# A token tower's finish rearranged: runs of sixteen tokens per partition, with base and weights sent through DRAM

## What is computed

```
h = _L0_tok_ref(x, ...)
h = h + _L0_attn_ref(_layernorm(h), ...)
h = h + _L0_ffn_ref(_layernorm(h), ...)     # = h + (xf + y)
# in _L0_ffn_ref, with xf the normalised tokens:
probs = softmax(xf @ Wr + br);  topk_w, topk_idx = top_k(probs, 2)
topk_w = topk_w / max(topk_w.sum(-1), 1e-9)
y = sum over the token's 2 experts e of  topk_w[e] * (gelu(xf @ W1[e] + b1[e]) @ W2[e] + b2[e])
```

## Time and profile before

| | us |
|---|---|
| median of three runs | 203.77 (203.3 to 203.94) |
| profiled execution, its own time | 204.18 |
| its span, first to last instruction | 202.4 |
| mean granted clock of TensorE | 0.875 of full |

### The profile page before, as it was taken

The page is one execution under the profiler, slowest core; times in us unless marked ns, Lnnn a source line. Parts: engine busy times, 40 slices in busy tenths (PEclk is TensorE's granted clock), DMA queues, the critical chain, the costliest instruction groups (busy, mean ns, idle before and its releaser), DMA issues.

```text
span 202.4 us, 3206 instructions
## 1 busy us (share of the span) xinstructions
PE 139.4 (69%) x792; PEld 100.0 (49%) x792; DVE 86.1 (43%) x289; ACT 74.5 (37%) x224; POOL 112.2 (55%) x154
## 2 busy tenths in 40 slices
PE   0429979999899566936189079999999999910000
PEld 0314324564565354535074059878777999910000
DVE  4261030454585485292698202545433322310183
ACT  2102124426444071130403035656566677700330
POOL 4293003130538777877777304777777777775250
PEclk9999999999999995795579856999999999995555
DMA  3999999999999921011011122444444421000877
GB/s 110 329 372 369 306 365 388 387 387 384 387 385 313 322 121 53 27 49 55 31 43 53 47 60 75 112 109 120 117 109 113 119 64 42 10 10 13 227 196 198
DMA packets 28948, 35.31 MB, mean 174 GB/s; under 512 B 3019, under 2 KB 18551, under 8 KB 28804
## 3 DMA queue, kind: packets, MB, share of 16 engines
q1 hardware_dynamic: 26328, 30.84, 47.3%
q0 software_dynamic: 2560, 4.27, 6.7%
q10 hardware_dynamic: 44, 0.01, 0.0%
HBM read 11.35 MB, written 24.81 MB: 179 GB/s over the span
## 4 chain that ended last, share of the span: by engine, by line
PE 45%; POOL 21%; issue 10%; DVE 10%; DMA 7%; ACT 2%; SPq 1%; ACTq 1%; DVEq 0%; POOLq 0%
PE bank L1075 13%; POOL slots L471 12%; PE bank L1065 11%; PE bank L919 9%; POOL parts L485 3%; PE bank L1052 3%; PE bank L904 3%; DMA work_a<-parts 3%; PE bank L909 3%; POOL root L456 2%; DVE work_c L854 2%; DMA rows<-in_L_tok_conv_b_dram 2%; POOL root_tab L421 1%; DMA slots<-stage,slot_of 1%; POOL root L464 1%
## 5 line engine op out<-in xcount | busy, mean ns | idle before, releaser
L485 POOL DMA_INDIRECT parts<-work_d,xt x48 | 47.2, 983 | 24.8 <-DVE work_d L837 16.0
L471 POOL DMA_INDIRECT slots<-stage,slot_of x32 | 32.4, 1011 | 11.0 <-issue 10.7
L585 ACT ACTIVATE act_hT<-bank,tile_b 128x128 f32<-128x128 f32 x96 | 30.1, 364 | 20.6 <-PE bank L1065 20.4
L1075 PE MATMUL bank<-w_sb,act_hT 128*128 (+1 forms) x192 | 32.8, 295 | 1.6 <-issue 0.6
L1075 PEld LDWEIGHTS bank<-w_sb,act_hT 128*128 128x128 f32 x192 | 26.0, 196 | 7.4 <-issue 6.9
L837 DVE TENSOR_TENSOR work_d<-bank,fb_bc 128x128 f32<-128x128 f32 x48 | 14.0, 292 | 35.9 <-PE bank L1075 35.9
L919 PE MATMUL bank<-x1T,convw_sb 128*128 128x512 f32 x48 | 23.2, 628 | 0.6 <-ACT x1T L532 0.4
L1065 PE MATMUL bank<-xtT,tile_w 128*128 128x128 f32 x128 | 21.4, 294 | 0.3 <-issue 0.3
L1065 PEld LDWEIGHTS bank<-xtT,tile_w 128*128 128x128 f32 x128 | 18.5, 209 | 0.6 <-issue 0.5
L1052 PE MATMUL bank<-ident,xt 128*128 128x128 f32 x48 | 13.9, 290 | 6.2 <-DMA xt<-slots 6.2
L575 ACT ACTIVATE xtT<-bank 128x128 f32<-128x128 f32 x48 | 13.3, 278 | 9.7 <-PE bank L1052 9.7
(11 more groups left out here) (181 smaller groups left out, 220.5 us busy)
## 6 DMA issues: line engine op xcount, KB each, us to landing
slots<-zero_rows SPq DMA_DIRECT2D x3, 4224.0 KB, 29.6
slots<-zero_rows SPq DMA_DIRECT2D x1, 5280.0 KB, 17.3
xt<-slots SPq DMA_DIRECT2D x48, 66.0 KB, 1.9
w_sb<-in_L_ffn_W_dram SPq DMA_DIRECT2D x1, 2048.0 KB, 16.7
fb_bc<-in_L_ffn_b_dram SPq DMA_DIRECT2D x1, 1024.0 KB, 7.0
work_b<-parts SPq DMA_DIRECT2D x4, 256.0 KB, 4.0
work_a<-parts SPq DMA_DIRECT2D x4, 256.0 KB, 5.8
out_dram<-work_c SPq DMA_DIRECT2D x4, 256.0 KB, 2.4
```

What stands on the lines that cost most here:

```text
L471: pool.indirect_dma_start(out=slots, out_offset=bass.IndirectOffsetOnAxis(ap=slot_of[:, g, k, s:s + 1].bitcast(U32), axis=0), in_=stage[:, ...
L485: pool.indirect_dma_start(out=parts, out_offset=bass.IndirectOffsetOnAxis(ap=xt[:, u, ROW_PLACE:ROW_PLACE + 1].bitcast(U32), axis=0), in_= ...
L585: last = act.activation(act_hT[:, b, c, :], bank[2 + b][:, c * P:(c + 1) * P], ACT.Gelu, bias=tile_b1[:, c, j:j + 1])
L1075: last = pe.matmul(bank[5 + j % 2][:, 0:D], act_hT[:, b, c, :], flat(w2_sb[:, expert_of(j), c, :]), start=(c == 0), stop=(c == 1))
```

## The change

The finish now gives each partition 16 tokens in a row (token 16 p + r), 8 KB of DRAM, in `CHUNKS` = 4 chunks of four tokens (2 KB per partition). `base` and `w_top` have the other layout, so SP writes them to DRAM tensors `base_rows` and `w_rows` ahead of its load of tile 16, and reads them back in the new layout, into `h1T` and `w_run`, ahead of its load of tile 32. First choices are loaded from SP's queue, second choices from ACT's. ACT scales all 16 blocks by w1; DVE computes base + w0 * first for all 16; POOL adds the two results for three chunks, DVE for the last.

```diff
+        w_run = sb("w_run", [P, T // P, TOPK])
...
+        RUN = T // P
+        CHUNKS = 4
+        CROWS = RUN // CHUNKS
+        base_run, first_run, second_run, scaled_run, sum_run, out_run = h1T, work_a, work_b, work_c, h0T, base
+
+        def run_rows(ap, c):
+
+            return ap.rearrange("(p r) d -> p (r d)", p=P)[:, c * CROWS * D:(c + 1) * CROWS * D]
+
+        def load_parts(eng, k, buf):
+
+            for u in range(U):
+                eng.wait_ge(placed[u], 16 * (TILES // U))
+            for c in range(CHUNKS):
+                eng.dma_start(buf[:, c, :], run_rows(parts[k * T:(k + 1) * T, :], c)).then_inc(parts_in[k][c], 16)
...
                 if j == 0:
                     sp.wait_ge(rows_out, 16 * TOPK * SEQS)
+                if j == U:
+                    sp.wait_ge(base_sum, GROUPS)
+                    sp.dma_start(base_rows.rearrange("(b p) d -> p b d", p=P),
+                                 base[:].rearrange("p g (s d) -> p (g s) d", d=D)).then_inc(base_out, 16)
+                    sp.wait_ge(w_ready, 1)
+                    sp.dma_start(w_rows.rearrange("(b p) k -> p b k", p=P), w_top[:]).then_inc(base_out, 16)
+                if j == FULL:
+                    sp.wait_ge(base_out, 32)
+                    sp.dma_start(base_run[:].rearrange("p g n -> p (g n)"),
+                                 base_rows.rearrange("(p r) d -> p (r d)", p=P)).then_inc(base_in, 16)
+                    sp.dma_start(w_run[:].rearrange("p r k -> p (r k)"),
+                                 w_rows.rearrange("(p r) k -> p (r k)", p=P)).then_inc(base_in, 16)
                 if j >= U:
                     sp.wait_ge(placed[u], 16 * (j // U))
                 sp.dma_start(xt[:, u, :], slots[bass.ds(row, P), :]).then_inc(xt_in[u], 16)
...
-            for k, buf in ((1, work_b), (0, work_a)):
-                for g in range(GROUPS):
-                    sp.dma_start(by_seq(buf[:, g, :]), both[k, :, g * GS:(g + 1) * GS, :]).then_inc(parts_in[k][g], 16)
+            load_parts(sp, 0, first_run)
+            tokens = out.rearrange("b t d -> (b t) d")
+            for c in range(CHUNKS):
+                sp.wait_ge(y_out, c + 1)
+                sp.dma_start(run_rows(tokens, c), out_run[:, c, :]).then_inc(stored, 16)
...
-            for g in range(GROUPS):
-                pool.wait_ge(scaled_y, g + 1)
-                most = slice(0, (GS - 1) * P)
-                pool.tensor_tensor(work_d[:, g, most], work_c[:, g, most], base[:, g, most], ALU.add).then_inc(summed, 1)
+            for c in range(CHUNKS - 1):
+                pool.wait_ge(scaled_y, c + 1)
+                pool.wait_ge(summed, c + 1)
+                pool.tensor_tensor(out_run[:, c, :], scaled_run[:, c, :], sum_run[:, c, :], ALU.add).then_inc(y_out, 1)
...
+            load_parts(act, 1, second_run)
+            act.wait_ge(base_in, 32)
+            for c in range(CHUNKS):
+                act.wait_ge(parts_in[1][c], 16)
+                for i in range(CROWS):
+                    last = act.activation(blocks(scaled_run[:, c, :], i), blocks(second_run[:, c, :], i), ACT.Copy,
+                                          scale=w_run[:, c * CROWS + i, 1:2])
                 last.then_inc(scaled_y, 1)
...
+            dve.wait_ge(base_in, 32)
+            for c in range(CHUNKS):
+                dve.wait_ge(parts_in[0][c], 16)
+                for i in range(CROWS):
                     last = dve.scalar_tensor_tensor(
+                        out=blocks(sum_run[:, c, :], i), in0=blocks(first_run[:, c, :], i),
+                        scalar=w_run[:, c * CROWS + i, 0:1], in1=blocks(base_run[:, c, :], i), op0=ALU.mult, op1=ALU.add)
+                last.then_inc(summed, 1)
+            dve.wait_ge(summed, CHUNKS)
+            dve.wait_ge(scaled_y, CHUNKS)
+            dve.wait_ge(y_out, CHUNKS - 1)
+            dve.tensor_tensor(out_run[:, CHUNKS - 1, :], scaled_run[:, CHUNKS - 1, :], sum_run[:, CHUNKS - 1, :],
+                              ALU.add).then_inc(y_out, 1)
```

More of the change, by code:

```diff
@@ L63, in tower_kernel @@
     parts = nc.dram_tensor("parts", [TOPK * T, D], F32).ap()
+    base_rows = nc.dram_tensor("base_rows", [T, D], F32).ap()
+    w_rows = nc.dram_tensor("w_rows", [T, TOPK], F32).ap()
     with ExitStack() as ctx:
@@ L231, in tower_kernel @@
         onehot_tile, b1_psum, b1_ready, t_w1 = map(sem, ("onehot_tile", "b1_psum", "b1_ready", "t_w1"))
+        w_ready, base_out, base_in = map(sem, ("w_ready", "base_out", "base_in"))
         parts_in = [[sem(f"parts{k}_in{g}") for g in range(GROUPS)] for k in range(TOPK)]
-        base_sum, base_ready, stored, scaled_y, summed, y_out = map(sem, ("base_sum", "base_ready", "stored", "scaled_y", "summed", "y_out"))
+        base_sum, stored, scaled_y, summed, y_out = map(sem, ("base_sum", "stored", "scaled_y", "summed", "y_out"))
         def blocks(ap, s):
@@ L371, in _ @@
                 sp.dma_start(xt[:, u, :], slots[bass.ds(row, P), :]).then_inc(xt_in[u], 16)
-            for u in range(U):
-                sp.wait_ge(placed[u], 16 * (TILES // U))
-            both = parts.rearrange("(k b p) d -> k p b d", k=TOPK, p=P)
-            for k, buf in ((1, work_b), (0, work_a)):
-                for g in range(GROUPS):
-                    sp.dma_start(by_seq(buf[:, g, :]), both[k, :, g * GS:(g + 1) * GS, :]).then_inc(parts_in[k][g], 16)
-            tokens = out.rearrange("b t d -> t b d")
-            for g in range(GROUPS):
[L382 to L385, removed]
+            load_parts(sp, 0, first_run)
[3 more added lines that the diff above has]
+                sp.dma_start(run_rows(tokens, c), out_run[:, c, :]).then_inc(stored, 16)
+            sp.wait_ge(stored, 16 * CHUNKS)
         @block.gpsimd
@@ L589, in _ @@
             experts(gelu=gelu, evacuate_x=evacuate_x)
-            act.wait_ge(base_ready, 1)
-            for g in range(GROUPS):
-                act.wait_ge(parts_in[1][g], 16)
-                for s in range(GS - 1):
-                    last = act.activation(blocks(work_c[:, g, :], s), blocks(work_b[:, g, :], s), ACT.Identity,
-                                          scale=w_top[:, g * GS + s, 1:2])
+            load_parts(act, 1, second_run)
[5 more added lines that the diff above has]
+                                          scale=w_run[:, c * CROWS + i, 1:2])
                 last.then_inc(scaled_y, 1)
@@ L840, in _ @@
             experts(load_expert=load_expert, add_b2=add_b2, copy_w1=copy_w1)
-            dve.wait_ge(base_ready, 1)
-            for g in range(GROUPS):
-                dve.wait_ge(parts_in[1][g], 16)
-                last = dve.scalar_tensor_tensor(
-                    out=blocks(work_d[:, g, :], GS - 1), in0=blocks(work_b[:, g, :], GS - 1),
-                    scalar=w_top[:, g * GS + GS - 1, 1:2], in1=blocks(base[:, g, :], GS - 1), op0=ALU.mult, op1=ALU.add)
-            link(last)
-            for g in range(GROUPS):
-                dve.wait_ge(parts_in[0][g], 16)
-                dve.wait_ge(summed, g + 1)
-                for s in range(GS):
-                    last = dve.scalar_tensor_tensor(
-                        out=blocks(work_c[:, g, :], s), in0=blocks(work_a[:, g, :], s), scalar=w_top[:, g * GS + s, 0:1],
-                        in1=blocks(work_d[:, g, :], s), op0=ALU.mult, op1=ALU.add)
-                last.then_inc(y_out, 1)
+            dve.wait_ge(base_in, 32)
+            for c in range(CHUNKS):
+                dve.wait_ge(parts_in[0][c], 16)
+                for i in range(CROWS):
+                    last = dve.scalar_tensor_tensor(
+                        out=blocks(sum_run[:, c, :], i), in0=blocks(first_run[:, c, :], i),
[6 more added lines that the diff above has]
+                              ALU.add).then_inc(y_out, 1)
         @block.tensor
```

4 lines of the change are left out of this document (1 added, 3 removed).

## The result

The changed kernel takes 215.48 us in the median of four runs (213.69 to 215.94), the kernel before in the same comparison 203.54 us (four runs). The ratio is 1.0588, 95% interval 1.0501 to 1.0674: slower, and beyond the range. The profiled execution took 215.18 us, its span is 213.4 us (before 202.4).

| stretch | before, us | changed, us | difference |
|---|---|---|---|
| start to the first scatter to `parts` | 122.98 | 122.37 | -0.6 |
| first to last scatter (48 tiles) | 61.64 | 70.54 | +8.9 |
| SP's first load of the finish to the end of the span | 15.6 | 18.3 | +2.7 |

The account below looks back on a forecast made before the run. It took PE (45%) and POOL (21% of the span) to carry the end, POOL saturated from tile 13. Span: 202.4 + 0.0 (finish) + 2.5 (stall) + 1.1 (clock) = 206.0 us; median 207.4 us, range 203.2 to 211 us.

Parts of the forecast that it names:

- 128 x 16 ns = 2.0 us for each engine: Ahead of tile 16: time to write `w_rows` in 2048 pieces of 8 bytes, 2.0 us, from a line through two larger piece sizes.
- my upper bound: Ahead of tile 16: `w_rows` takes at most 4.3 us, the price of 2048 pieces of 512 bytes.
- the small pieces are slow: Rival at tile 16: `w_rows` takes 4.3 us or more, stall 5.7 us or above, +7.2 us, 211 us; chance 0.15.
- at twice that, 215 us: Further case of the slow-pieces rival: `w_rows` at twice 4.3 us gives 215 us; within that rival's chance of 0.15.
- 1.05 + 4.8: Ahead of tile 16: `base_rows` takes 1.05 us from issue to data, then 4.8 us to write 1 MB.
- POOL's lag: At tile 13: 0.62 us between b2 addition's end and scatter, absorbing 0.6 us of the stall, later slack 0.2 us.
- the 1.1 taken: After tile 16's stall: half of the 2.3 us that a fall of PE's clock would cost, +1.1 us.
- Tile 32's reads: At tile 32: reading `base_rows` back, 2.7 us, costs nothing because SP is ahead; without that cover up to 2 us.
- the exclusion: In the finish: DVE stands while POOL adds because they share ports, making the cycle 2.5 us a chunk instead of 1.4.
- 199.8 + 2.6: End of the finish: closing addition done at 199.8 us, last store 2.6 us more, span ending at 202.4 us, no gain.
- 0.4 us less of the 3.0: Last store: 2 KB pieces take 0.67 instead of 1.05 us, shortening the 3.0 us behind its issue.
- The rival without exclusion: In the finish: DVE and POOL do not block each other, finish -3.3 us, with the stall 204.1 us; chance 0.12.

Follow-up runs that it names:

- e1: Changed kernel without the weights' way through DRAM, DVE copying `w_top` to `w_run` on chip; 207.93 us, ratio 1.0240 to the kernel before.
- e14: Changed kernel with 64 bytes a token written to `w_rows`, side by side, 8 of them read back; 212.65 us, ratio 1.0472.
- e10: Kernel before, old layout, with second choices loaded by ACT, DVE's sums of base and first choices, all closing additions on DVE; 202.32 us, ratio 0.9954.
- e5: Changed kernel with the 8-byte pieces of `w_rows` 512 bytes apart in DRAM; 213.07 us, ratio 1.0473.
- e2: Changed kernel without `base`'s way through DRAM, the finish reading `base` in its old layout; 211.0 us, ratio 1.0398.
- e9: e7 with each chunk a contiguous block of 512 tokens in DRAM instead of 2 KB out of every 8; 201.11 us, ratio 0.9890.
- e7: e3 with POOL's three additions given to DVE; 203.37 us, ratio 0.9989 to the kernel before.
- e13: Changed kernel, complete, with DRAM writes and reads behind the last tile's load, POOL's additions on DVE, and contiguous chunks; 201.65 us, ratio 0.9921.
- e3: Changed kernel with neither `base` nor weights sent through DRAM, both used in the old layout; 205.31 us, ratio 1.0102.
- e4: Kernel before plus only the change's four DMAs to and from DRAM, their data unused; 212.47 us, ratio 1.0466.
- e12: Changed kernel, DRAM trips behind last tile load, POOL's additions on DVE, `w` written in 128-byte pieces and read in 8-byte pieces; 202.77 us, ratio 0.9993.

## Why the prediction was wrong

**Direction and place were right, the size was not.** Of the prediction's own steps:

- **The step that failed: "128 x 16 ns = 2.0 us for each engine"** for `w_rows`. It measured 6.2 us, 4.2 more, and e1 shows that these pieces make 7.5 of the 8.9 us. The line through 512 and 2112 bytes was drawn on to 8 bytes, where it has no support; my upper bound, the price of 2048 pieces of 512 bytes, was no bound either, since 8-byte pieces cost more than 512-byte ones. The two rows taken as a check on small pieces were reads of 128 pieces, and reads are the cheap side (e14). The rival "the small pieces are slow" is what happened, at 1.4 times its 4.3 us. That its "at twice that, 215 us" meets the measured time is luck: at 6.2 us its own sum gives about 213 us, and the rest is the finish, in which it saw no loss.
- `base_rows` was right: 5.5 us from issue to landing, against 1.05 + 4.8. It was issued 0.5 us earlier and landed 0.35 us sooner after that, and the tile's own load took 0.45 us behind the small pieces instead of 0.85. So tile 16's data came at 144.85 instead of 141.9 us: 4.2 - 0.85 - 0.4 = 3.0 us later than forecast.
- The profiled execution of the changed kernel was 0.6 us ahead at its first scatter (122.37 us). That is spread and not the change: e10, whose front is that of the kernel before, has 122.51 us, e5 123.05. Counted from the first scatter the same landing is 0.6 us later still, so tile 16's turn was 6.8 us late, where I had 3.3.
- POOL's lag took back 0.35 us (the addition ended 0.28 instead of 0.62 us ahead of the scatter), not 0.8.
- The clock fell "for certain", as in that rival. From tile 16's turn to the end of tile 13's addition it was 2.49 us, before 1.45, and from tile 13's scatter to 16's 1.3 us more: 2.4 us, most of it at half clock, against the 1.1 taken. Shorter stalls were followed by the low level too: after 2.62 us in e2 the windows from 142 to 146 us show 0.50, after 2.28 us in e14 0.63 and 0.52. So to take half of the clock's price for a stall of 3.3 us was too little. Sum for the tiles: 6.8 - 0.35 + 2.4 = 8.9 us, as measured.
- The 1 MB's own effect on PE's pace, 1.4 to 2.0 us in e1, was not in the prediction at all: it counted bandwidth and queue order, not register loads that wait beside the transfer. In the changed kernel it adds nothing, since it lies inside the wait for tile 16; taking away the small pieces uncovers it.
- Tile 32's reads cost nothing, as said. e14 shows how little more it takes: at 7.2 instead of 5.5 us PE stood 2.42 us there.
- **The finish** came out as three misses. The first chunk was at DVE after 4.63 us, not 3.4 (+1.2; e9 shows the 8 KB interval). DVE took 8.26 us, not 9.6 (-1.3): the exclusion is there (three DVE instructions lengthened to 1.35 to 1.37 us, additions of 1.26 to 1.29 us as taken for POOL), but POOL's starts lie 1.84 and 2.08 us apart instead of 2.5. The 0.32 us a block was too dear, since the 5.10 us that it came from hold one lengthened block; four unhindered blocks take 1.14 us (e7). And DVE's next chunk had begun when POOL's addition did. The end lay 5.4 us behind DVE, not 2.6 (+2.8). **This is the second step that failed:** "199.8 + 2.6" has only the last store behind DVE, and POOL's DRAIN ended later than any store. The "0.4 us less of the 3.0" did not come either: the last store's wait ended 2.7 us behind DVE (SP's DRAIN, 210.7 us), before 2.6, and stores landed 2.4 us after their issue in both. With contiguous chunks they landed after 2.0 us (e13). 1.2 - 1.3 + 2.8 = 2.7 us, the loss of the finish. The rival without exclusion (-3.3 us) needed a DVE free of POOL; with POOL's additions gone (e7) the gain on e3 was 3.0 us, 2.5 of it from the DRAIN and 0.5 from a DVE that no longer stands but adds itself.

The Trainium skill's rule on the ports of DVE and GpSimd (SBUF — State Buffer, "SBUF: two separate sides") agrees with this trace: one DVE instruction was lengthened for each of POOL's three additions, to 1.35 to 1.37 us. That the cycle was shorter than 2.5 us is a matter of my sum and not of the rule. The Trainium skill's rule on transfers under 512 bytes (DMA: Bandwidth & Descriptors, "Specifications") named the direction: the pieces did cost more than the upper bound taken from 512-byte rows. It gives no price for such a write, and no run shows that a read-modify-write is behind it. Nor does it order small pieces among themselves: 64-byte pieces, under the same limit, took 2.2 us (e14).

**Where the gain of the larger pieces went:** in the changed kernel into the slow start, and then behind POOL's DRAIN. The shorter finish exists (13.42 us in e13 against 15.6), once chunks are contiguous, POOL ends early and the trips lie behind the last load; half of it is to be had without any change of layout (e10: 14.49 us). By the medians e13 gains 1.7 us on the kernel before and e10 0.8 us.

## What to carry to other kernels

A change of layout through DRAM is priced by its smallest pieces on the written side: look for the row with the fewest bytes a piece, and if the trace has none near it, take the case where it is twice the dearest known piece into the range (here it was 1.4 times). Then place such a trip where the queue behind it has nothing urgent; the same four DMAs cost 8.9 us ahead of tile 16 and 0 to 0.7 us behind tile 47. At the end of a program, read the closing DRAINs as well as the last store: an engine's last instruction can set the end though its data are long there.

## What the runs showed of the hardware

- 2048 writes of 8 bytes to DRAM held the queue's next transfers for 6.2 us, with DMA engines shown occupied at 52 to 74 GB/s. 512 bytes apart: 3.9 us; in pieces of 64 bytes: 2.2 us. 2048 reads of 8 bytes, 64 bytes apart, landed 2.4 us behind the 1 MB ahead of them (e14).
- POOL's closing DRAIN ended 6.6 to 6.7 us after POOL's last instruction in the kernel before, the changed kernel, e4, e7 and e10, whether that was an addition or a scatter. Whether it is owed to the scatters was not tried.
- Loading a register on PE or DVE, 0.30 us, took up to 0.97 and 1.16 us while 1 MB was written at 260 to 285 GB/s.
- An issue can hold SP. Behind the 1 MB write the issue of `w_rows` took 2.11 us with 2048 pieces and 1.85 us with 128 (e12), with nothing ahead 0.39 us (e2); so it is the 1 MB ahead that holds it and not its own pieces. The load behind both took 3.18 us, behind the 1 MB alone up to 1.96 us (e1), 0.33 us otherwise.
- Loads of 2 KB pieces started at 145 and 289 GB/s in two successive microseconds when the pieces lay 8 KB apart, and at 285 and 373 GB/s when contiguous.
